# The second token tile of the gated layer's last product, moved into the next step of a written-out order, on one Trainium2 core

## What is computed

```
x  = x + tanh(g_xattn) * attention(layernorm(x), ctx)      # 16 heads of width 32, 256 context rows
      q, o projections: rows rounded to 8-bit integers with one scale per token
x  = x + tanh(g_ffn) * ffn(layernorm(x))
      g, u = qx @ Wg.T, qx @ Wu.T          # 512 -> 1408, rows and weights rounded to fp8
      t = silu(g) * u
      qt, st = round_fp8(t / (max|t| / 448))   # one scale per token
      y = (qt @ Wd.T) * st                     # 1408 -> 512, "the down product"
```

## Time and profile before

| | |
|---|---|
| median of three runs | 570.88 us |
| the profiled execution's own time | 571.12 us |
| its span, first to last instruction | 569.3 us |
| busy: PE / DVE / ACT / POOL | 449.5 / 487.7 / 461.4 / 232.8 us |
| mean granted PE clock | 0.955 of full speed |
| chain that ended last: DVE / POOL / ACT / issue / PE / DMA | 36 / 14 / 14 / 13 / 10 / 5 % |

### The profile page before, as it was taken

How to read it: one execution, slowest core, us unless ns; L and a number is a source line. 1 busy time by engine, 2 the same in 40 slices (tenths; PEclk the granted TensorE clock), 3 DMA queues, 4 the chain that set the end, 5 groups by cost and what they waited for, 6 DMA issues and landing times.

```text
span 569.3 us, 9874 instructions
## 1 busy us (share of the span) xinstructions
PE 449.5 (79%) x3030; PEld 272.7 (48%) x3030; DVE 487.7 (86%) x1254; ACT 461.4 (81%) x1129; POOL 232.8 (41%) x212
## 2 busy tenths in 40 slices
PE   0397496988998899889988988899889975963854
PEld 0274374555545554555455544554555443531321
DVE  5999789988798889888988798889888987699993
ACT  5779799998988798989888888898989886963350
POOL 4432262004653455246434642555246422541620
PEclk9999887999999999999999999999999998895967
DMA  8942352112114221322132113221321121000001
GB/s 259 387 139 79 98 149 56 38 57 38 56 27 94 62 57 26 89 68 57 27 104 52 57 26 84 74 55 27 91 65 20 27 53 30 20 0 16 20 17 74
DMA packets 61060, 39.51 MB, mean 69 GB/s; under 512 B 47568, under 2 KB 53712, under 8 KB 61008
## 3 DMA queue, kind: packets, MB, share of 16 engines
q1 hardware_dynamic: 56256, 27.47, 18.4%
q0 software_dynamic: 3328, 11.41, 6.3%
q10 hardware_dynamic: 1424, 0.01, 0.1%
HBM read 23.87 MB, written 4.19 MB: 49 GB/s over the span
## 4 chain that ended last, share of the span: by engine, by line
DVE 36%; POOL 14%; ACT 14%; issue 13%; PE 10%; DMA 5%; DVEq 0%; POOLq 0%; SPq 0%; ACTq 0%
POOL up L464 5%; POOL up L454 4%; DVE ts L1482 3%; ACT prob L655 3%; DVE q L1204 3%; POOL x L433 3%; DVE q_last L1305 3%; DVE prob L1305 2%; ACT q_last L655 2%; PE bank_h L887 2%; DVE rows L1421 2%; DVE t_sb L1199 2%; DVE stats L1411 2%; DMA t_sb<-in_L_ffn_w_up_dram,index 2%; ACT rows L571 2%
## 5 line engine op out<-in xcount | busy, mean ns | idle before, releaser
L454 POOL TENSOR_TENSOR up<-up,wgu_scale 128x512 f32<-128x512 f32 (+1 forms) x42 | 52.0, 1239 | 81.8 <-ACT up L635 81.8
L664 ACT ACTIVATE probT<-bank_h 128x512 f32<-128x512 f32 x128 | 68.5, 587 | 1.3 <-PE bank_h L887 0.7
L655 ACT ACTIVATE prob<-prob,neg_max 128x256 f32<-128x256 f32 x128 | 63.3, 498 | 5.5 <-DVE neg_max L1305 5.5
L655 ACT ACTIVATE q_last<-q_last,neg_max 128x256 f32<-128x256 f32 x128 | 63.5, 499 | 2.2 <-DVE neg_max L1305 2.1
L469 POOL TENSOR_TENSOR x<-x,y 128x512 f32<-128x512 f32 x14 | 19.9, 1423 | 101.6 <-DVE y L1495 101.6
L464 POOL TENSOR_TENSOR up<-gate,up 128x512 f32<-128x512 f32 (+1 forms) x42 | 59.5, 1423 | 3.7 <-DVE gate L1360 1.5
L1305 DVE CUSTOM_DVE_ANT_0 prob<-bank_h,mask_sb 128x256 f32<-128x256 f32 x128 | 47.4, 420 | 12.9 <-PE bank_h L828 12.9
L887 PE MATMUL bank_h<-ident,prob 128*128 128x128 f32 x256 | 39.9, 291 | 12.8 <-ACT prob L655 12.7
L1305 DVE CUSTOM_DVE_ANT_0 q_last<-bank_h,mask_sb 128x256 f32<-128x256 f32 x128 | 47.4, 417 | 0.0
L914 PE MATMUL bank_o<-probT,v_sb 128*32 128x256 f32 x512 | 36.0, 400 | 14.0 <-DVE v_sb L1233 8.0
L562 ACT ACTIVATE mag<-t_sb,ts 128x512 f32<-128x512 f32 (+1 forms) x42 | 28.6, 680 | 20.1 <-DVE ts L1487 12.6
(11 more groups left out here) (237 smaller groups left out, 1209.0 us busy)
## 6 DMA issues: line engine op xcount, KB each, us to landing
x_in<-in_x_dram SPq DMA_DIRECT2D x8, 512.0 KB, 3.6
c_in<-in_ctx_dram SPq DMA_DIRECT2D x8, 512.0 KB, 3.8
out_dram<-x POOLq DMA_DIRECT2D x7, 512.0 KB, 3.8
mask_sb<-in_mask_BxSxS_ff_dram SPq DMA_DIRECT2D x8, 256.0 KB, 3.0
t_sb<-in_L_ffn_w_down_dram SPq DMA_DIRECT2D x2, 704.0 KB, 5.5
t_sb<-in_L_ffn_w_down_dram POOLq DMA_DIRECT2D x2, 704.0 KB, 6.8
kf<-in_L_xattn_wq_dram SPq DMA_DIRECT2D x1, 1024.0 KB, 10.8
wkT<-in_L_xattn_wk_dram SPq DMA_DIRECT2D x1, 1024.0 KB, 13.5
```

The costliest lines, as they stand in the source:

```text
L454: pool.tensor_tensor(up[:, c % 2, 0:w], up[:, c % 2, 0:w], wu_scale[:, off:off + w], ALU.mult).then_inc(f["u_scaled"], 1)
L655: ins = act.activation(prob_of[slot4][:, t, :], prob_of[slot4][:, t, :], ACT.Exp, bias=neg_max[:, slot4, t:t + 1], scale=-1.0, accum_out=r ...
L664: act.activation(probT[:, (slot + 3) % 4, :, :].rearrange("p a b -> p (a b)"), HEAD_BANK[(slot + 3) % 4][:, :], ACT.Copy).then_inc(s["turn ...
```

## The change

The program of every step now gets the blocks of the step before as well (`p`), and these parts of **tile 1** move from the end of step b into the first part of step b+1: `t_mag`, `t_sum`, `t_sub`, `t_turn`, both halves of the down product, `y2_scale`, `out_add` and the store. Step 2 has no such part to take over, and the tail takes over that of step 7. Tile 0's stay in their step.

The result of the down product is no longer added into `x2`. Tile 0 uses `y2`, tile 1 a free slice of `raw_o`; `out_add` writes the sum there, and each tile is stored alone (two transfers of 256 KB in place of one of 512 KB; semaphores `stored_0`, `stored_1`). That slice of `raw_o` is the one into which `x_int` writes, so `x_int` now waits for the store of tile 1.

```diff
+        y2_of = [y2[:, :], raw_o[:, 2, :]]
...
                 def x2_add(slot):
-                    need(pool, s["stored"], 16 * B2)
+                    if B2:
+                        pool.wait_ge(s["out_ready"], 1 + 2 * B2)
...
                 def out_add(slot):
                     t = (slot - 13) // 2
+                    if not D:
+                        return
                     pool.wait_ge(f["y2_ready"], 1 + 2 * B2 + t + 1)
-                    pool.tensor_tensor(x2[:, t, :], x2[:, t, :], y2[:, :], ALU.add).then_inc(f["out_ready"], 1)
+                    if A:
+                        pool.tensor_tensor(y2_of[t], x2[:, t, :], y2_of[t], ALU.add).then_inc(s["out_ready"], 1)
...
                 def out_store(slot):
+                    if A:
+                        pool.wait_ge(s["out_ready"], 1 + 2 * B2 + t + 1)
+                        pool.dma_start(out[bass.ds(b - 2, 1)][:, t * P:(t + 1) * P, :].rearrange("o p c -> p (o c)"), y2_of[t]).then_inc(s[f"stored_{t}"], 16)
...
                 def x_int(slot):
                     for t in range(NT):
                         act.wait_ge(s["x_rounded"], 2 * b + t + 1)
+                        if b > 2:
+                            act.wait_ge(s["stored_1"], 16 * (b - 2))
...
                 def y2_scale(slot):
                     dve.wait_ge(f["d_ps"], 1 + 2 * B2 + t + 1)
+                    if A:
+                        need(dve, s[f"stored_{t}"], 16 * B2)
+                        if t == 1:
+                            dve.wait_ge(s["xT_ready"], 32 * (b + 1))
+                        dve.scalar_tensor_tensor(y2_of[t], G_BANK[:, :], ts_[:, 1, t:t + 1], wd_scale[:, :], ALU.mult,
+                                                 ALU.mult).then_inc(s["y2_ready"], 1)
+                        return
```

All four lists of all five engines are written anew. ACT's steady list shows the kind of edit (its first and last calls):

```diff
-            def steady_step_order(k):
-                k.head_probT(0); k.o_int(0); k.x_centre(0); k.head_exp(0); k.head_exp(1); k.k_out_0(3); k.x_round(2)
-                k.x_int(2); k.head_exp(2); k.head_exp(3); k.head_probT(1); k.head_probT(2); k.head_probT(3)
+            def steady_step_order(k, p):
+                p.t_mag_0(12); p.t_mag_1(12); k.head_probT(0); p.t_mag_2(13); k.o_int(0); k.x_centre(0); k.head_exp(0)
+                k.head_exp(1); k.k_out_0(3); k.x_round(2); k.group_oT(1); k.head_exp(2); k.head_exp(3); k.head_probT(1)
+                k.head_probT(2); k.head_probT(3); k.head_probT(4); k.x_int(2); k.x2_mag_0(3); k.x2_mag_1(3)
...
+                k.head_exp(13); k.head_exp(14); k.head_probT(13); k.head_probT(14); k.head_probT(15); k.o_round(15)
+                k.head_exp(15)
```

More of the change, by code:

```diff
@@ L371, in _ @@
             for b in range(2, NB):
-                steady_step_order(blocks(b))
-            tail_order(blocks(NB))
-            sp.wait_ge(s["stored"], 16 * NB)
+                steady_step_order(blocks(b), blocks(b - 1))
+            tail_order(blocks(NB), blocks(NB - 1))
+            for t in range(NT):
+                sp.wait_ge(s[f"stored_{t}"], 16 * (NB - 2))
+            sp.wait_ge(s["stored"], 32)
         @block.gpsimd
@@ L728, in first_step_order @@
             def first_step_order(k):
[L729 to L731 removed]
+                k.unit_mag_0(0); k.unit_mag(2); k.gate_tanhs(2); k.unit_copy(3); k.pro_round_q(0); k.unit_copy(5)
+                k.unit_mag(4); k.unit_mag(6); k.x_centre(0); k.unit_mag(8); k.unit_copy(7); k.pro_round_o(3)
@@ L1514, in first_step_order @@
[L1514 to L1522 removed]
+                k.unit_scale_0(0); k.unit_scale(0); k.unit_round_0(0); k.unit_round(3); k.pro_scale_q(0); k.x_stats(0)
@@ new lines, in second_step_order @@
+            def second_step_order(k):
+                k.x_stats(0); k.head_mask(0); k.head_mask(1); k.head_mask(2); k.head_mask(3); k.x_scales(2)
+                k.unit_scale(0); k.unit_scale(2); k.unit_round(1); k.unit_round(3); k.head_mask(4); k.head_mask(5)
+                k.unit_scale(4); k.head_mask(6); k.head_mask(7); k.unit_round(5); k.unit_round(7); k.head_mask(8)
+                k.head_mask(9); k.sx_copy(7); k.q_scale_0(7); k.head_mask(10); k.head_mask(11); k.unit_scale(6)
+                k.unit_scale(8); k.q_scale_1(8); k.unit_scale(10); k.unit_round(9); k.unit_round(11); k.v_evac(11)
+                k.v_evac(12); k.head_mask(12); k.head_mask(13); k.head_mask(14); k.head_mask(15); k.unit_round(13)
@@ L1523, in second_step_order, with steady_step_order @@
                 k.o_norm(14); k.o_max(14); k.o_norm(15); k.o_max(15); k.o_scales(15)
-            def steady_step_order(k):
-                k.x_stats(0); k.head_mask(0); k.head_mask(1); k.x_scales(2); k.y_scale(1); k.head_mask(2)
+            def steady_step_order(k, p):
+                k.x_stats(0); p.t_sum_0(12); p.t_sub_0(12); p.t_sum_1(12); p.t_sub_1(12); p.t_sum_2(13); p.t_sub_2(13)
+                k.head_mask(0); k.head_mask(1); k.head_mask(2); k.x_scales(2); p.y2_scale(15); k.y_scale(1)
```

291 lines of the change are left out of this document (150 added, 141 removed).

## The result

The changed kernel takes **574.88 us** (median of five runs, 573.70 to 575.21) against 570.88 for the kernel before: a ratio of 1.0062, with a 95% interval of 1.0041 to 1.0084. It is 0.6% slower. I had forecast 566.7 us. The range, 554 to 575, just holds the time, but the sign was wrong. The profiled execution took 573.7 us, 2.6 more than that of before. It is the fastest of the change's five, so its rows account for 2.6 us, while the medians differ by 4.0.

The account below looks back on a forecast made before the run. No engine alone bounds it: PE, DVE and ACT are 89% full, the rest waits. Terms -0.9 - 1.0 - 1.2 - 0.5 - 0.8 = -4.4 against 571.12 give 566.7 us; range of all 554 to 575.

Parts of the forecast that it names:

- The walk from mark to mark: Steady step cut at three marks of DVE's timeline, each stretch walked through the new lists: 56.7 us a step.
- Tile 1's factors to the x2 factors: Boundary stretch, where the moved part now stands: 20.5 us, with DVE idle 2.4 us.
- X to Q: From x2 factors ready (X) to tile 0's t factors ready (Q): 19.4 us, 18.3 before, two masks added.
- Q to R: From tile 0's t factors ready (Q) to tile 1's (R): 16.8 us, 11.6 before, nearly without waits.
- the long step: One steady step before the change, 58.5 us, 2.4 longer with the same work; half credited, -1.2 us.
- The last step's credit of 1.0 us: Last steady step has no `x_stats`, so its rounding starts about 1 us earlier: -1.0 us.
- The prologue: Step 1: `x_plus_bias` leaves the place between two weight loads: -0.5 us, between -2.5 and +2.
- The tail: After the steady steps, `head_score(8)` goes ahead of one projection, tile 1 ahead of its heads: -0.8 us, between -2 and +2.
- The store: `x_int` waits for tile 1's store: costs nothing, by a margin of 0.3 to 1.1 us.
- The store rival: Tile 1's store lands late and holds up `x_int` and the x2 magnitudes: about 578 us, chance 0.12.
- The opened boundary: Transposes land at 2.4 us, scores are ready, boundary and score waits go: steps 54.7, about 556 us, chance 0.33.
- My own sign for the forecast: At the step's boundary, DVE waits at L1414 for the second output projection for over 1 us.

Follow-up runs that it names:

- e5: The changed kernel with POOL's `x_plus_bias` behind `x2_var` and also waiting for the first x2 rounding: 571.67 us, ratio 1.0014 to the kernel before.
- e11: The changed kernel with `x_plus_bias` of steps 2 to 7 cut to one column of 512: 571.47 us, ratio 1.0013 to the kernel before.
- e1: The kernel before with the changed kernel's lists for steps 0 and 1 alone: 567.8 us, ratio 0.9958.
- e2: The changed kernel with the old steady and tail orders on all engines; new buffers, stores, `x_int` wait and first-step lists kept: 566.36 us, ratio 0.9932.
- e3: Old steady order with only tile 1's calls moved to the next step's start; tail and first steps as changed: 615.05 us, ratio 1.0778.
- e10: The changed kernel with POOL's store of tile 1 behind `x_plus_bias` instead of ahead: 581.58 us, ratio 1.0205 to the kernel before.

## Why the prediction was wrong, point by point

- **The walk from mark to mark was right in two parts of three.** Tile 1's factors to the x2 factors: 20.5 us forecast, 14.95 to `x2_stats` and 5.53 from there measured, 20.5. Idle there: 2.4 forecast, 2.4 measured. But two errors cancel: `x2_stats` came 0.5 us earlier than I walked, and the norm took 5.5 and not 5.0. X to Q: 19.4 forecast, 19.4 measured. Q to R: 16.8 forecast, **17.4** measured, of which `t_sum_0` beside POOL is 0.4, and the idle is 0.82 where I had nearly none. The step was forecast at 56.7 and is 57.36: over six steps +4.0.
- **"No arithmetic is removed or added, so DVE's work of a step stays near 50.5 us" is the step that failed.** It is the sentence on which the forecast of no loss rests. A step of 56.7 with 50.5 busy leaves 6.2 idle. The trace has 6.25 idle and 51.1 busy, so the whole miss of the plain step, 0.65 us, is DVE's busy time. The arithmetic is the same, yet DVE is busy 1.1 us longer than before, of which 0.75 are instructions that meet POOL's and are counted as busy while they wait. e5 and e11 show that 1.2 us of a plain step hang on where POOL's `x_plus_bias` falls, enough to bring it back to 56.2. (The kernel before pays 0.75 of this kind too, its centring being 1.62 and not 0.88 us, so the new order without it is no faster than the old one with it.) I had costed the store's issue ahead of it at nothing, on POOL's low busy share. What it moved was POOL's phase against DVE, by 0.44 us.
- **The total used the long step twice.** I compared a plain walk, 56.7, with the average of before, 56.85, which already holds the 2.4 us of the long step (and 1.8 of the first step and 0.5 of the last), and then took half of the 2.4 off again. Against the plain step of 56.1 my own walk said +0.6, that is slower. Counted rightly, my terms give six steps of 56.7 and 1.2 for half the long step, 341.4 or +0.3, and with -1.0, -0.5 and -0.8 a total of -2.0, not -4.4. Measured, steps above the plain length add 1.7 us in all, against 4.7 before. So 3.0 us of extra did go, more than I had credited, and the six plain lengths cost 7.7 (1.29 each): +4.7.
- **The last step's credit of 1.0 us did not come** (57.3, like the others). Without `x_stats` DVE reaches the first rounding sum earlier and waits 1.0 us for ACT's magnitude; later it waits 3.3 us for the down product.
- **The prologue was mis-sized in our favour**: -0.5 forecast, -2.8 measured in the trace, -2.4 by the times of e1. The tail: -0.8 forecast, +0.6 measured in this trace, which is at the low end. Nine traces with the change's tail list have 94.3 to 97.0 us, 95.7 on average, and four with the old one 93.2 to 94.0. So the tail probably costs about 2 us, for which no experiment was made. The account of the profiled execution is -4.4, +4.0 for the plain steps, +3.9 for the credits that I had taken off and the steps above plain, -2.3 for the prologue and +1.4 for the tail: +2.6, as measured.
- **The store** was rightly costed at nothing, and its margin was mis-sized. I had 0.3 to 1.1 us between the end of `x_int` and X. In the change the landing can slip by 1.7 to 2.1 us before X is missed, of which only the first 0.2 to 0.6 pass without a wait on ACT. It landed sooner than the row I took (2.4 us as the median of these 256 KB stores, not 3.8; at the old place, in e2, they took up to 4.2). That is close to the 2.6 us that the Trainium skill ("DMA: Bandwidth & Descriptors", the anatomy of one DMA) gives by its formula, an estimate. The store rival's mechanism is e3 and e10; it does not decide in the change as written, but it takes back a part of e5 and e11.
- **The opened boundary** did not happen: the transposes did land at 2.4 us, as its condition asked, but five in a row on SP take 1.2 us or more each, and the idle at the boundary stayed at 2.2 us (before 2.25; the 1.5 in the prediction left out the smaller gaps). My own sign for the forecast, over 1 us of waiting at L1414 for the second output projection, did not show either: it was 0.5. The length of the step, 57.4, was within the 56 to 57.5 that I had given.

## What to carry to other kernels

Here the length of a DVE instruction with two SBUF inputs depended on what POOL did beside it: 0.69 us alone, up to 1.37 beside it. When an edit shifts one engine's list, list which instruction pairs newly overlap, and price each at the remaining length of the blocking instruction; do not take "same work" as "same busy time". Compare a walk of a plain step with a plain step, never with an average that holds an exception. Before counting on slack (here ACT's behind `x_int`), see whether the next gain uses it up. And take a change apart: here its prologue and its buffers together were worth 0.7%, and its main idea, with the orders written for it, cost 1.3%.

## What was unexpected in the hardware

DVE's instructions are not stretched in proportion beside POOL; those that read one of their inputs from PSUM, and the statistics, are not lengthened at all in these traces. Masks stay at 0.42 us, the gate product at 0.75 and a `BN_STATS` at 0.67 to 0.70 beside POOL's instructions, while a product of two SBUF tensors goes from 0.69 to 1.37, and one of 128x2 from 0.13 to 1.02, to end when POOL's instruction does. The Trainium skill ("SBUF — State Buffer", "Who interferes with whom") has this rule: a DVE instruction with two SBUF inputs and a GpSimd instruction that reads SBUF exclude each other for a whole instruction, and so do a DVE instruction in one of the two-port modes, which `tensor_scalar` can enter, and any of GpSimd. The traces agree (two centrings 0.88 us alone, 2.07 beside `x_plus_bias`). It is the rule that spoke against this change, and I had not weighed it: no rival of the prediction names it.
